# Routed mixture: seven sequences chosen and placed ahead of the tiles, and 85 tiles in one stream

## The chip, the cores and the metric

The kernel is one program on one core of a Trainium2 chip. The metric is device time in microseconds (us) of one launch. One execution was also taken by the hardware profiler; its trace is what the views below are read from.

## The reference, cut to what matters

The model carries eight sequences of 512 tokens by 128 features through ten layers: rwkv, attention, mixture, alibi, attention, mixture, lightning attention, **routed mixture**, differential attention, **routed mixture**. Only the routed mixture (layers 8 and 10, both with the same weights) is changed. It computes, in the reference's terms (tokens x after a layer norm):

```
logits = norm(x) @ w_gate                       # 8 experts
two largest logits -> softmax of the two        # TOP_K = 2
x += sum over the two chosen experts e of
     weight * ((silu(z @ w1[e]) * (z @ w3[e])) @ w2[e])
```

with w1, w3 of 128 by 256 and w2 of 256 by 128 for each of the eight experts. 4096 tokens, two experts each, make 8192 rows of expert work.

## The kernel before, in words

**Sorting instead of masking.** `routed_block` writes each token's normalized row twice into a DRAM buffer, sorted by expert, reads it back in tiles of 128 rows that all belong to one expert, runs the expert on the tile, writes the results, gathers each token's two result rows, and adds them with their weights. The eight sequences are cut into three chunks of 3, 3 and 2 sequences (`Routed.SEQS`); each chunk has its own sorted buffer, results buffer and table, and 31, 31 and 23 tiles (`Routed.TILES`: two rows per token, and seven tiles more for experts that fill no whole tile), 85 in all.

**What is done to a sequence j.** VectorE: `statistics` (mean and variance), `shifted`; GpSimd: `token_scales`, a power for a group of sequences (`Routed.SCALED`: 1; 2; 3 and 4; 5 to 7); ScalarE: `tokens`, the normalized rows; TensorE: `head_turned`, four transposes; ScalarE `head_hi` and VectorE `head_lo` split them in a high and a low half; TensorE `gate`, eight small products; VectorE `chosen`: the two largest logits of each token, their index and one-hot rows, and `both`, the sum of the one-hots; TensorE `ranks`: how many rows of each expert come before a token, by products of `both` with a triangle and with ones; VectorE `placed`: the row in the sorted buffer (`row_idx`), and the running fill `run`; GpSimd `sort`: eight indirect DMAs that write the rows. After the last sequence of a chunk, VectorE `tabled` makes from the fill the table of tiles (which expert, which row), and `way_back` the indices of the gathers.

**What is done to a tile n.** SyncE `tile` loads it (ten slots, `SLOTS`); TensorE turns it (L4727); ScalarE copies it (L4822); TensorE `up` (L4735, w1 and w3 at once); ScalarE silu (L4828); VectorE `product_g` (L4997); TensorE turns g (L4743); ScalarE copies (L4834); TensorE `down` (L4751, two products); VectorE `result` (L5004) copies it into one of four slots for pairs of tiles; SyncE `pair` (L4648) stores pairs.

**Order.** Each engine runs its list strictly in the order written, and waits on semaphores. TensorE's list per tile is up(n), down(n-2), turn of tile n+2, turn of g(n-1); VectorE's is result(n-2), product_g(n). Ahead of tile 0 stand the gates, ranks and choices of sequences 0 to 4 (`AHEAD` = 5). Sequences 5, 6 and 7 are fitted in among the tiles of chunk 0 from tiles 1, 8 and 15 on (`WITHIN`, `due`): gate and next turn, choice, low half, ranks, placing, and the table, in six consecutive turns. Each chunk's loop has two more turns than tiles (`turns`), in which its last tiles drain; the next chunk begins with its table's expert and two turned tiles:

```
wait(t, vec_table, c, "row")
at_w = {0: expert_of(0)}
tile_turned(n0)
tile_turned(n0 + 1)
for i in turns(c):
```

SyncE, per chunk: `pads` (eight stores that blank the row after each expert's fill), the pairs up to eight tiles before the chunk's first, a wait for the sort, then per tile the load and the pairs up to twelve tiles back. GpSimd: scales 0 and 1, sort 0, sort 1, scales 2, sort 2, scales 3, sorts 3 to 7, one power for all weights (`seconds`), and then 64 gathers (`gathered`, L5119), those of a chunk behind its last stored pairs. VectorE adds the sequences back (`added`, L5011 and L5015) at tiles 45, 52, 59, 76 and 83, and the last three behind the stream. In the first of the two layers, `opening` prepares the next layer; in the last one, SyncE stores the finished sequences (`tokens_out`).

Of the kernel before, what the change touches and what calls it, by code (L numbers as in the profile page):

```python
# [18 lines left out]
F32 = mybir.dt.float32  # L19
# [8 lines left out]
P = 128  # L28
# [4477 lines left out]
class Routed:  # L4506
# [13 lines left out]
    ADDED = {(1, 14): 0, (1, 21): 1, (1, 28): 2, (2, 14): 3, (2, 21): 4}  # L4520
    WITHIN = {5: (0, 1), 6: (0, 8), 7: (0, 15)}
    OPENED = 2
    AHEAD = 5
# [8 lines left out]
def routed_block(core, name, store):  # L4532
# [7 lines left out]
    PARTS = 6  # L4540
    WAY_BACK = 4
    chunk_of = lambda j: max(c for c in range(R.CHUNKS) if R.FIRST[c] <= j)
    last_of = lambda c: R.FIRST[c] + R.SEQS[c] - 1
    with ExitStack() as ctx:
# [5 lines left out]
        pe_rank, vec_shift, vec_table = steps("_ranks_tensor"), steps("_shift_vector"), steps("_table_vector")  # L4550
# [18 lines left out]
        both, place, picked = sb("both", [P, NQ * 8], F32R), sb("place", [P, NQ, 8]), sb("picked", [P, 2 * NQ, 8])  # L4569
        row_at, row_idx, run = sb("row_at", [P, NSEQ, 2 * NQ]), sb("row_idx", [P, NSEQ, 2 * NQ], U32), sb("run", [P, 8])  # L4570
# [23 lines left out]

        def due(c, i):

            for j, (of, first) in R.WITHIN.items():
                if of == c and first <= i < first + PARTS:
                    return j, i - first
            return None, None  # L4600

        turns = lambda c: range(R.TILES[c] + 2)
# [16 lines left out]
        def _(sp):  # L4619
# [47 lines left out]
            for c in range(R.CHUNKS):  # L4667
# [7 lines left out]
                for t in range(R.TILES[c]):  # L4675
                    tile(c, t)
                    if n0 + t >= 12:
                        m = pairs_to(m, n0 + t - 12)
                    if store and (c, t - SLOTS - 1) in R.ADDED:
                        tokens_out(R.ADDED[c, t - SLOTS - 1])  # L4680
                        shown.append(R.ADDED[c, t - SLOTS - 1])
# [8 lines left out]
        def _(t):  # L4690
# [17 lines left out]
            def ranks(j):  # L4708
                pe_rank.start()
                if j == 0:  # L4710
                    t.wait_ge(fixed, 5)
# [548 lines left out]
```

## Time and profile before

| | |
|---|---|
| runs timed | 3: 2580.46, 2586.67, 2590.57 us; median 2586.67 |
| profiled execution, own time | 2577.03 us |
| its span, first to last instruction | 2574.9 us |
| TensorE busy | 2186.4 us (85%) |
| VectorE busy | 1669.4 us (65%) |
| ScalarE busy | 1275.9 us (50%) |
| GpSimd busy | 1389.3 us (54%) |
| mean granted TensorE clock | 0.908 |
| first routed mixture | from about 1543 to 1804 us of the span |
| second routed mixture | from about 2317 us to the end |

Times in rows are us from the span's start. PE is TensorE, DVE VectorE, ACT ScalarE, POOL GpSimd, SPq SyncE's queue; PEclk is the granted clock as a share of full speed. Busy shares are means over ten unlike layers; the change is inside two of them.

### The profile page before, as it was taken

Reading aid. Unit: us, or ns where it says so; the run is one execution under the profiler, and the core shown is the slowest. Engines: PE = TensorE matmul, PEld = TensorE weight load, DVE = VectorE, ACT = ScalarE, POOL = GpSimd, SP = SyncE. Lnnn points to the kernel's source line nnn. Section 1 sums busy time; section 2 is a strip of 40 time slices with the busy share of each in tenths; the row PEclk is TensorE's granted clock in tenths of the full one; section 3 lists DMA queues with packets and bytes.
Section 4 is the critical chain, followed back from the end, with each engine's and each line's share of the span. In section 5 each row is a group of like instructions: output and inputs, shape, how many; then the busy total and the mean of one; then the engine's idle time right before and its main releaser. Section 6 shows DMA issues by size and latency. Waiting matters only on the chain. (4 is left out here: it accounts for less than half of the span.)

```text
span 2574.9 us, 41201 instructions
## 1 busy us (share of the span) xinstructions
PE 2186.4 (85%) x11902; PEld 1314.4 (51%) x11902; DVE 1669.4 (65%) x4560; ACT 1275.9 (50%) x2246; POOL 1389.3 (54%) x1353
## 2 busy tenths in 40 slices
PE   4567998999779979998999995984899999985894
PEld 3344565666665646664444444653444444434663
DVE  6865775677557747766666655543687877755543
ACT  4543454333344543335766643453477767763452
POOL 5933754343336544426666656445666766627435
PEclk8788798899788999999999995997899999995997
DMA  1000110322011111221000003332000000003333
GB/s 50 0 3 16 46 44 3 124 86 80 20 30 39 38 52 75 99 81 42 1 1 1 1 2 117 90 105 75 13 1 1 1 1 0 1 1 114 92 108 104
DMA packets 113863, 113.22 MB, mean 44 GB/s; under 512 B 22776, under 2 KB 93560, under 8 KB 113400
## 3 DMA queue, kind: packets, MB, share of 16 engines
q1 hardware_dynamic: 105464, 93.92, 12.1%
q0 software_dynamic: 8192, 16.79, 2.3%
q8 instruction: 99, 1.62, 0.3%
q14 instruction: 108, 0.88, 0.1%
HBM read 72.50 MB, written 25.43 MB: 38 GB/s over the span
## 5 line engine op out<-in xcount | busy, mean ns | idle before, releaser
L2332 DVE TENSOR_REDUCE l_diffneg_max<-psum 128x1 fp32r<-128x512 f32 x512 | 335.5, 685 | 89.6 <-PE psum L2070 86.0
L2247 ACT ACTIVATE l_diffweights<-psum 128x1024 f32<-128x1024 f32 x256 | 261.8, 1025 | 127.5 <-PE psum L2099 126.4
L2070 PE MATMUL psum<-l_diffkz,l_diffQ 128*128 128x512 f32 (+1 forms) x512 | 234.4, 476 | 3.2 <-DVE l_diffneg_max L2332 2.1
L2871 ACT ACTIVATE l_lightswapped<-psum 32x512 f32<-32x512 f32 x304 | 178.7, 588 | 101.1 <-DVE l_lightturned L2963 97.7
L1597 DVE TENSOR_REDUCE l_attn0neg_max<-psum 128x1 fp32r<-128x512 f32 x256 | 167.4, 683 | 51.5 <-PE psum L1328 48.8
L5119 POOL DMA_INDIRECT l_moe1yb<-results,l_moe1back_idx x128 | 122.7, 958 | 134.1 <-DVE l_moe1back_idx L4991 57.7
L1503 ACT ACTIVATE l_attn0weights<-psum 128x1024 f32<-128x1024 f32 x128 | 130.2, 1022 | 116.1 <-PE psum L1350 116.0
L4296 ACT ACTIVATE l_moe0s<-psum 128x512 f32<-128x512 f32 x144 | 85.8, 596 | 200.0 <-PE psum L855 183.0
L1724 POOL TENSOR_TENSOR l_attn0half_sums<-l_attn0weights 128x2048 f32<-128x2048 f32 x30 | 137.2, 4574 | 86.9 <-ACT l_attn0weights L1503 86.9
L4735 PE MATMUL psum<-l_moe1w,l_moe1zt 128*128 x340 | 183.8, 624 | 0.0
L5107 POOL DMA_INDIRECT sorted<-l_moe1rows,l_moe1row_idx x128 | 124.0, 969 | 79.9 <-DVE l_moe1run L4939 44.1
L175 POOL TENSOR_TENSOR settled<-powers 128x1 f32<-128x1 f32 x97 | 24.2, 250 | 257.9 <-DVE l_alibimv L702 70.7
L223 POOL TENSOR_TENSOR l_moe0ex<-powers,l_moe0hot 128x32 f32<-128x32 f32 x14 | 76.1, 5439 | 156.6 <-DVE l_moe0hot L274 156.6
L4751 PEld LDWEIGHTS psum<-l_moe1w,l_moe1gt 128*128 128x128 f32 x680 | 95.7, 193 | 121.0 <-issue 121.0
L4217 PE MATMUL psum<-l_moe0g,l_moe0w_raw 128*128 128x512 f32 x288 | 148.9, 602 | 7.5 <-ACT l_moe0out_sb L4271 7.5
L2070 PEld LDWEIGHTS psum<-l_diffkz,l_diffQ 128*128 128x128 f32 (+1 forms) x512 | 95.1, 186 | 111.5 <-issue 64.2
L5004 DVE COPY l_moe1y<-psum 128x128 f32<-128x128 f32 x170 | 49.4, 291 | 149.1 <-PE psum L4751 143.5
L2485 POOL TENSOR_TENSOR l_difflow_rows<-l_diffwhole,l_diffmarks 128x512 fp32r<-128x512 f32 x63 | 65.5, 1040 | 139.1 <-ACT l_diffwhole L2231 136.5
L2113 PE MATMUL psum<-l_diffweights,x 128*32 128x512 f32 x1024 | 137.0, 608 | 0.0
L4751 PE MATMUL psum<-l_moe1w,l_moe1gt 128*128 x680 | 108.5, 283 | 27.5 <-DVE l_moe1y L5004 22.4
L4371 DVE TENSOR_TENSOR l_moe0sc<-l_moe0s,l_moe0bcs 128x512 f32<-128x512 f32 x128 | 93.6, 731 | 58.5 <-ACT l_moe0s L4296 48.2
L2099 PE MATMUL psum<-l_diffQ,l_diffkz 32*128 32x512 f32 (+1 forms) x512 | 129.5, 494 | 1.5 <-DVE l_diffneg_max L2332 0.9
(602 smaller groups left out, 6055.7 us busy)
## 6 DMA issues: line engine op xcount, KB each, us to landing
l_moe0bcs<-gate_rows SPq DMA_DIRECT2D x64, 512.0 KB
l_moe1xt<-sorted SPq DMA_DIRECT2D x170, 64.0 KB, 1.8
results<-l_moe1y SPq DMA_DIRECT2D x82, 128.0 KB, 2.0
l_attn0Q<-l_attn0q_hi SPq DMA_DIRECT2D x128, 64.0 KB, 2.0
l_moe1w<-in_moe_w SPq DMA_DIRECT2D x6, 1024.0 KB, 8.8
l_attn0Q<-l_attn0q_lo SPq DMA_DIRECT2D x64, 64.0 KB, 2.0
sorted<-l_moe1spare SPq DMA_DIRECT2D x54, 64.0 KB, 1.6
l_moe0w_raw<-in_moe_w SPq DMA_DIRECT2D x20, 128.0 KB, 4.7
```

The lines of the kernel that those rows point to most:

```text
L1503: nc.scalar.activation(weights[:, tt, 2 * pair:2 * pair + 2, :], ps[:, S[m % 2]:S[m % 2] + 2, :], ACT.Exp, scale=SCALE).then_inc(act_exp.s ...
L1597: nc.vector.tensor_reduce(neg_max[:, n % 2, st, hh:hh + 1], ps[:, bank_of(("max", n, b)), :], AXX, ALU.max, negate=True).then_inc(vec_max. ...
L1724: nc.gpsimd.tensor_tensor(halves[:, a, :, :], weights[:, 2 * a, :, :], weights[:, 2 * a + 1, :, :], ALU.add).then_inc(pool_sum.sem, pool_s ...
L2070: nc.tensor.matmul(ps[:, bank, :], Q[rows, n % 4, st * P:(st + 1) * P], kz[rows, n % 4, hh, :], start=True, stop=True).then_inc(pe_max.sem ...
L2099: ins = nc.tensor.matmul(ps[:, S[m % 2] + h, :], kz[rows, n % 4, hh, tt * P:(tt + 1) * P], Q[rows, n % 4, :], start=True, stop=True)
L2113: ins = nc.tensor.matmul(ps[strip(hh), O, :], V[:, j % 2, tt, g * PER_GROUP + hh, :], weights[:, tt, hh, :], start=(tt == 0), stop=(tt == ...
L2247: nc.scalar.activation(weights[:, tt, 2 * pair:2 * pair + 2, :], ps[:, S[m % 2]:S[m % 2] + 2, :], ACT.Exp, scale=SCALE).then_inc(act_exp.s ...
L2332: nc.vector.tensor_reduce(neg_max[:, n % 2, st, row:row + 1], ps[:, bank_of(("max", n, b)), :], AXX, ALU.max, negate=True).then_inc(vec_ma ...
L2871: copy = lambda to, frm: nc.scalar.activation(to, frm, ACT.Copy)
L4217: ins = nc.tensor.matmul(ps[:, OUT, :], weights_in.raw[:, c:c + P], g[:, n % G_RING, h, :], **ends)
L4735: nc.tensor.matmul(ps[:, H[n % 2], :], zt[:, n % 2, :], w[:, bass.ds(w_at, 4 * P)], start=True, stop=True).then_inc(pe_up.sem, pe_up.step( ...
L4751: ins = nc.tensor.matmul(ps[:, Y, 0:P], gt[:, n % 2, h * P:(h + 1) * P], w[:, bass.ds(w_at + (4 + h) * P, P)], start=h == 0, stop=h == 1)
```

## The change

- `chosen`, `ranks` and `placed` of sequences 0 to 6 stand ahead of tile 0, and so do the gate and turn of sequence 7. Among the tiles remain the choice of sequence 7 (tile 1), its ranks (tile 3) and placing (tile 4), the tables of chunks 1 and 2 (tiles 6 and 10) and the ways back (tiles 2, 13, 16). `WITHIN`, `due` and `turns` go.
- `placed` gets a semaphore of its own (`vec_place`) and a fill per chunk (`run[:, c, :]`); the next choice waits for the ranks to have read `both`, and no longer for the placing. The copy of `base` into `run` goes.
- The tiles are one loop of 85 on TensorE, ScalarE and VectorE; only two drain turns at the end remain. The wait for a chunk's table stands where its first expert is read.
- `ranks` takes five products in place of eight: `both` has eight zero columns behind it, and the totals come out of the same products.
- GpSimd: scales 2 between sort 0 and sort 1, scales 3 between sort 1 and sort 2. VectorE: the statistics come earlier in the list, table 0 stands behind the choice of sequence 3, and the shifts of 5 to 7 behind table 0.
- SyncE: pairs are stored ahead of the load in a tile's turn, not behind it; finished sequences are stored eleven tiles after their adding back across chunks, so that in the last layer three, not one, are stored among the tiles.

```diff
+    ALL = sum(TILES)
+    CHOSEN, RANKED, PLACED = 1, 3, 4
+    TABLED = {6: 1, 10: 2}
+    WAYS_BACK = {2: 0, 13: 1, 16: 2}
+    ADDED = {45: 0, 52: 1, 59: 2, 76: 3, 83: 4}
...
                 for t in range(R.TILES[c]):
-                    tile(c, t)
                     if n0 + t >= 12:
                         m = pairs_to(m, n0 + t - 12)
+                    tile(c, t)
...
-                wait(t, chooser.vec_gate, j - 1, "comb")
+                wait(t, vec_place, j - 1, "comb")
                 wait(t, chooser.vec_gate, j, "both")
-                nc.tensor.matmul(ps[:, RANKS, 0:32], less[:, :], both[:, :], start=True, stop=False, skip_group_check=True)
-                for q in range(1, NQ):
-                    nc.tensor.matmul(ps[:, RANKS, 8 * q:32], ones[:, :], both[:, 0:32 - 8 * q], start=False, stop=q == NQ - 1,
-                                     skip_group_check=True)
-                for q in range(NQ):
-                    ins = nc.tensor.matmul(ps[:, RANKS, 32:40], ones[:, :], both[:, 8 * q:8 * q + 8], start=q == 0, stop=q == NQ - 1,
+                nc.tensor.matmul(ps[:, RANKS, 0:40], less[:, :], both[:, :], start=True, stop=False, skip_group_check=True)
+                for q in range(1, NQ + 1):
+                    ins = nc.tensor.matmul(ps[:, RANKS, 8 * q:40], ones[:, :], both[:, 0:40 - 8 * q], start=False, stop=q == NQ,
                                            skip_group_check=True)
...
             head_turned(3)
             gate(3)
+            ranks(2)
             head_turned(4)
-            ranks(3)
             gate(4)
-            ranks(4)
             head_turned(5)
...
+            for j in (4, 5, 6):
+                ranks(j - 1)
+                gate(j + 1)
+                if j + 2 < NSEQ:
+                    head_turned(j + 2)
+            ranks(6)
+            at_w = {}
+            for n in range(R.ALL):
...
+                up(n, at_w[n])
...
+                if n >= 2:
+                    down(n - 2, at_w.pop(n - 2))
+                if n + 2 < R.ALL:
+                    tile_turned(n + 2)
+                if n >= 1:
+                    g_turned(n - 1)
+                if n == R.RANKED:
+                    ranks(NSEQ - 1)
...
             placed(0)
+            statistics(3)
             head_lo(1)
             shifted(2)
-            statistics(3)
             statistics(4)
             chosen(1)
             head_lo(2)
+            statistics(5)
             placed(1)
+            shifted(3)
+            shifted(4)
+            statistics(6)
+            statistics(7)
+            head_lo(3)
             chosen(2)
             placed(2)
+            head_lo(4)
+            chosen(3)
             tabled(0)
...
             for j in range(5, NSEQ):
                 shifted(j)
...
+            for j in (4, 5, 6):
+                head_lo(j + 1)
+                chosen(j)
+                placed(j - 1)
+            placed(6)
+            for n in range(R.ALL):
+                if n >= 2:
+                    result(n - 2)
+                product_g(n)
+                if n == R.CHOSEN:
+                    chosen(NSEQ - 1)
+                if n == R.PLACED:
+                    placed(NSEQ - 1)
+                if n in R.TABLED:
+                    tabled(R.TABLED[n])
+                if n in R.WAYS_BACK:
+                    way_back(R.WAYS_BACK[n])
...
             sort(0)
+            token_scales(2)
             sort(1)
-            token_scales(2)
-            sort(2)
             token_scales(3)
-            for j in range(3, NSEQ):
+            for j in range(2, NSEQ):
                 sort(j)
```

## Rows read from the trace of the kernel before

**Rows 1.** Time line, VectorE, first mixture: products of tiles 0, 30, 32, 44, 61, 63. Columns: start, duration, engine, line, operation, tiles, count, [idle before, releaser].

```profile
1600.96 0.42 DVE L4997 TENSOR_TENSOR l_moe1g<-l_moe1s,psum 128x256 f32<-128x256 f32 x1 [3.86 <-ACT l_moe1s L4828]
...
1665.41 0.41 DVE L4997 TENSOR_TENSOR l_moe1g<-l_moe1s,psum 128x256 f32<-128x256 f32 x1
...
1671.89 0.42 DVE L4997 TENSOR_TENSOR l_moe1g<-l_moe1s,psum 128x256 f32<-128x256 f32 x1 [0.58 <-PE psum L4743]
...
1691.46 0.41 DVE L4997 TENSOR_TENSOR l_moe1g<-l_moe1s,psum 128x256 f32<-128x256 f32 x1
...
1726.75 0.41 DVE L4997 TENSOR_TENSOR l_moe1g<-l_moe1s,psum 128x256 f32<-128x256 f32 x1
...
1733.25 0.42 DVE L4997 TENSOR_TENSOR l_moe1g<-l_moe1s,psum 128x256 f32<-128x256 f32 x1 [0.58 <-PE psum L4743]
```

**Rows 2.** Time line, VectorE, second mixture: products of tiles 20, 30 and 31.

```profile
2420.43 0.41 DVE L4997 TENSOR_TENSOR l_moe1g<-l_moe1s,psum 128x256 f32<-128x256 f32 x1
...
2438.61 0.41 DVE L4997 TENSOR_TENSOR l_moe1g<-l_moe1s,psum 128x256 f32<-128x256 f32 x1
...
2445.04 0.42 DVE L4997 TENSOR_TENSOR l_moe1g<-l_moe1s,psum 128x256 f32<-128x256 f32 x1 [3.37 <-ACT l_moe1s L4828]
```

**Rows 3.** Windows: the head of the first mixture; clock behind POOL's busy time.

```profile
1543.00:1598.00 55.00, 23.58 (x101) 21.23 (x101) 32.56 (x253) 14.37 (x34) 38.38 (x44) 0.51 0.40 123
```

**Rows 4.** Time line, GpSimd, first mixture: first sort, second scale, last gathers.

```profile
1552.77 1.24 POOL L5107 DMA_INDIRECT sorted<-l_moe1rows,l_moe1row_idx  x1 [1.46 <-DVE l_moe1run L4939]
...
1572.97 1.70 POOL L5093 TENSOR_TENSOR l_moe1scale<-l_moe1var,powers 128x8 f32<-128x8 f32 x1
...
1774.99 0.94 POOL L5119 DMA_INDIRECT l_moe1yb<-results,l_moe1back_idx  x1 [5.18 <-DMA results<-l_moe1y]
```

**Rows 5.** Time line, VectorE, head of the first mixture: table 0 to sequence 3.

```profile
1571.11 0.17 DVE L4946 CAST l_moe1table<-l_moe1run 128x8 int32<-128x8 f32 x1
...
1574.77 0.28 DVE L4891 SCALAR_TENSOR_TENSOR l_moe1shift<-l_moe1mv,l_moe1scale 128x4 f32<-128x4 f32 x2
...
1578.51 0.69 DVE L4897 TENSOR_TENSOR l_moe1h_lo<-psum,l_moe1h_hi 128x512 fp32r<-128x512 f32 x1 [3.46 <-ACT l_moe1h_hi L4816]
...
1581.17 0.19 DVE L262 COPY l_moe1ex<-psum 128x32 f32<-128x32 f32 x1 [1.97 <-PE psum L216]
...
1583.32 0.19 DVE L4906 TENSOR_TENSOR l_moe1both<-l_moe1hots 128x32 fp32r<-128x32 f32 x1
...
1585.61 0.19 DVE L4931 TENSOR_TENSOR l_moe1place<-psum,l_moe1run 128x32 f32<-128x32 f32 x1 [1.41 <-PE psum L4719]
...
1586.49 0.16 DVE L4939 TENSOR_TENSOR l_moe1run<-l_moe1run,psum 128x8 f32<-128x8 f32 x1
```

**Rows 6.** Time line, TensorE: ranks' last products; turn of tile 31, second mixture.

```profile
1584.51 0.99 PE L4719 MATMUL psum<-l_moe1both,l_moe1ones 128*128 128x8 f32 x4
...
2441.53 0.30 PE L4727 MATMUL psum<-ident,l_moe1xt 128*128 128x128 f32 x1 [0.20 <-issue]
```

**Rows 7.** Time line, VectorE, first mixture: products of tiles 2, 3, 6, 7, 9.

```profile
1605.69 0.41 DVE L4997 TENSOR_TENSOR l_moe1g<-l_moe1s,psum 128x256 f32<-128x256 f32 x1
...
1608.47 0.41 DVE L4997 TENSOR_TENSOR l_moe1g<-l_moe1s,psum 128x256 f32<-128x256 f32 x1
...
1613.91 0.41 DVE L4997 TENSOR_TENSOR l_moe1g<-l_moe1s,psum 128x256 f32<-128x256 f32 x1
...
1618.13 0.41 DVE L4997 TENSOR_TENSOR l_moe1g<-l_moe1s,psum 128x256 f32<-128x256 f32 x1
...
1624.64 0.41 DVE L4997 TENSOR_TENSOR l_moe1g<-l_moe1s,psum 128x256 f32<-128x256 f32 x1
```

**Rows 8.** Time line, SyncE, second mixture: pads of chunk 1, loads from tile 31 on.

```profile
2422.69 8.15 SPq L4634 DMA_DIRECT2D sorted<-l_moe1spare  x8
...
2433.30 7.71 SPq L4640 DMA_DIRECT2D l_moe1xt<-sorted  x7
```

**Rows 9.** Page, DMA issues: tile loads, KB each, us to landing.

```profile
l_moe1xt<-sorted SPq DMA_DIRECT2D x170, 64.0 KB, 1.8
```

More of the change, by code:

```diff
@@ L4919, in placed @@
             def placed(j):
-                inc, wait_for = chooser.steps(d, j)
-                wait_for("both")
-                if j in R.FIRST:
-                    if j:
-                        wait(d, vec_table, chunk_of(j) - 1, "pads")
-                    v.tensor_copy(run[:, :], base[:, :]).then_inc(chooser.vec_gate.sem, chooser.vec_gate.step("begin"))
-                else:
-                    d.sem_inc(chooser.vec_gate.sem, chooser.vec_gate.step("begin"))
-                wait_for("begin")
+                vec_place.start()
+                inc = lambda ins, *key: ins.then_inc(vec_place.sem, vec_place.step(*key))
+                wait_for = lambda *key: wait(d, vec_place, j, *key)
+                c = chunk_of(j)
+                ahead = base[:, :] if j in R.FIRST else run[:, c, :]
                 wait(d, pe_rank, j, "rank")
+                wait(d, vec_place, j - 1, "comb")
                 found = ps[:, RANKS, 0:32].rearrange("p (q e) -> p q e", e=8)
-                inc(v.tensor_tensor(place[:, :, :], found, run[:, :].unsqueeze(1).to_broadcast([P, NQ, 8]), ALU.add), "place")
+                inc(v.tensor_tensor(place[:, :, :], found, ahead.unsqueeze(1).to_broadcast([P, NQ, 8]), ALU.add), "place")
                 wait_for("place")
@@ L4938, in placed @@
                 inc(v.tensor_copy(row_idx[:, j, :], row_at[:, j, :]), "row_idx")
-                inc(v.tensor_tensor(run[:, :], run[:, :], ps[:, RANKS, 32:40], ALU.add), "comb")
+                inc(v.tensor_tensor(run[:, c, :], ahead, ps[:, RANKS, 32:40], ALU.add), "comb")
             def tabled(c):
@@ L4944, in tabled @@
                 wait_for = lambda key: d.wait_ge(vec_table.sem, vec_table.done(c, key))
-                wait(d, chooser.vec_gate, last_of(c), "comb")
-                inc(v.tensor_copy(table[:, c, PAD_AT:PAD_AT + 8], run[:, :]), "pads")
-                inc(v.tensor_tensor(count[:, :], run[:, :], base[:, :], ALU.subtract), "count")
+                wait(d, vec_place, last_of(c), "comb")
+                inc(v.tensor_copy(table[:, c, PAD_AT:PAD_AT + 8], run[:, c, :]), "pads")
+                inc(v.tensor_tensor(count[:, :], run[:, c, :], base[:, :], ALU.subtract), "count")
                 wait_for("count")
@@ new lines, in _ @@
+            for j in (4, 5, 6):
[3 more added lines that the diff above has]
+            placed(6)
+            for n in range(R.ALL):
+                if n >= 2:
[9 more added lines that the diff above has]
+                    way_back(R.WAYS_BACK[n])
+                if n in R.ADDED:
+                    if R.ADDED[n] == 0:
+                        weighed()
+                    added(R.ADDED[n])
+                    if opening and R.ADDED[n] == 0:
+                        wait(d, vec_add, 0, "second")
+                        opening.statistics(d)
+                if opening and n == R.ALL - 1:
+                    opening.low(d, TOK)
+                    opening.weights_low(d)
```

158 lines of the change are left out of this document (48 added, 110 removed).

## The prediction

> **What bounds the kernel now.** The change touches only the routed mixture, which runs twice among the ten layers. I read the time line of each engine inside these two stretches; over the whole span the mixture is hidden behind averages. Call g(n) the start of tile n's gated product on VectorE: it is the beat of the tile stream.
>
> [rows 1] give the first mixture. Between g(32) and g(44) a tile costs (1691.46 - 1671.89)/12 = 1.63 us; 85 tiles at that beat would be 139 us. The real stream is slower in two places. Tiles 0 to 30 take 1665.41 - 1600.96 = 64.45 us where 30 beats are 48.9: 15.5 us lost. And at each seam between chunks two beats take 6.48 and 6.50 us in place of 3.26. [rows 2] show the same in the second mixture, where the first seam is 6.43 us for one beat. So the bound is the stream on TensorE, plus what VectorE puts between tiles, plus the drain and refill at the seams. Ahead of it lies the head, up to g(0), in which TensorE is granted 0.51 of its clock, the 1.2 GHz level for nearly all of it, and waits for short steps [rows 3]. Behind it lies the tail: GpSimd gathers, 16 pieces that wait for the last result [rows 4].
>
> **The change part by part.**
>
> *The head.* Seven sequences instead of five are chosen, ranked and placed before tile 0, and the gate's products of the eighth are made there. Steps from [rows 5], all at the head's slow clock: from shift to the low half 1578.51 - 1574.77 = 3.74; the low half 0.69; choosing, 1583.32 + 0.19 - 1581.17 = 2.34; from there to placing 2.10; placing, 1586.49 + 0.16 - 1585.61 = 1.04; a table, 1574.77 - 1571.11 = 3.66. The ranks' last four products take 0.99 [rows 6], 0.25 each; three fewer make the 2.10 into 1.35. On GpSimd a sort piece costs (1572.97 - 1552.77)/16 = 1.26 and the second scale 1.70 [rows 4].
>
> In the new order the second scale stands behind sort 0 alone: 1552.8 + 8 x 1.26 + 1.70 = 1564.6. VectorE waits for it with shift 3. From there: 3.74 to the low half of 3 (1568.3), 0.69 + 2.34 choosing 2 (1571.4), 1.35 + 1.04 placing it (1573.8), about 0.8 for the next turn (my estimate, part of the 3.74), 0.69 + 2.34 choosing 3 (1577.6), 3.66 for table 0 (1581.3). Only now does shift 5 stand in VectorE's order, though its scale was ready about 1577 (eight pieces and a scale after 1564.6); this is the new wait, and tokens, turn, high and low half of 5 follow it: 3.74, 1585.0. Then three rounds of low half, choice and placing, each 0.69 + 2.34 + 1.04 and 0.3 of waits = 4.4: 1598.1. Ranks 6, 1.35: 1599.5. TensorE turns tile 0 behind it, and from turn to product at the slow clock takes 2445.04 - 2441.53 = 3.51 [rows 2, 6]: g(0) at 1603.0 against 1600.96. **The head costs 2.0 us more in each mixture.** Bounds: 2 less (no waits inside the rounds, the first 0.8 hidden), 6 more (0.3 of waits becomes 1.5). The sort of chunk 0 is not the limit: 24 pieces and both scales end near 1587, and the tile lands well before 1599.
>
> *Tiles 0 to 30.* Before, three sequences' gate, turn, choice, ranks and placing and two tables fell among them. Now: one choice, one set of ranks, one placing, two tables and all ways back. [rows 7] price them: a choice stretches its beat to 2.78, so +1.15; placing with a table makes 4.22, so +2.6; the second, shorter table I put at +2.3. The way back right behind the choice gets 0.5 (between 0 and its length, about 1.15); the other two lie alone and fit the gap that VectorE has in a beat. Ranks with five products at the full clock 0.7, placing 0.3, the first tiles at the slow clock 0.3. Sum 7.85. Chunk 0 then takes 48.9 + 7.85 = 56.8: **7.7 us less per mixture.** Bounds of the insertions: 4 (what is only VectorE's is caught up again) and 12.
>
> *The seams.* The turns of tiles 31, 32 and 62, 63 no longer wait for the drain. But the queue of SyncE is in order: pads of the next chunk, 8.15 us, and pairs stand ahead of load 31, which goes out 2433.30 - 2420.43 = 12.9 after g(20) [rows 2, 8]; 1.8 to landing [rows 9] makes 14.7. The turn is wanted 3.5 before g(31), which is g(20) + 11 x 1.63 = 17.9, so at 14.4. I take a bubble of 0.6 (0 to 2). First seam: 6.48 becomes 3.86, 2.6 gained; in the second mixture 6.43 becomes 2.2, 4.2 gained. Second seam: adding back two sequences lies between g(51) and g(62) and gives SyncE time, no bubble: 3.2 in each.
>
> *The rest.* Pairs ahead of loads, not behind: loads run ten tiles ahead, nothing. The placing step's own semaphore and the copy of the base that goes: some 0.2 per placing, in VectorE's slack or in the 0.3 above. In the last layer two more stores of tokens leave in mid-stream; that puts two issues of about 1 us (the pads' 8.15/8) on SyncE ahead of loads that have slack. The tail moves with the last result as long as the gathers of chunk 1 are done: they had 5.18 us to spare [rows 4], and the pair of tile 61 comes up to 3 us later against the stream, so 2 stay. The first adding back may wait for its gather: 0.3 in each mixture. The tail itself is unchanged.
>
> Sum: first mixture -2.0 + 7.7 + 2.6 + 3.2 = 11.5, second -2.0 + 7.7 + 4.2 + 3.2 = 13.1, less 0.6: **24 us**. Against the profiled execution's own 2577.0 (span 2574.9 and 2.1 around it) that is 2553. The median of the runs shown, 2586.7, lies 9.6 above it, as does most of their spread (2580.5 to 2590.6); I forecast in the median's terms: 2586.7 - 24 = **2563**.
>
> On the clock: the rows say that the head runs at 1.2 GHz [rows 3], and that two beats behind the first table took 1624.64 - 1618.13 = 6.51 instead of 3.26 [rows 7], in which a gate and a turn (about 1.5 at the full clock) leave 1.7 unexplained but by a fallen clock. The Trainium skill (TensorE: Matmul & The Clock Gate, "Part 1: The HAM clock gate") has the throttled state as the default, which activity releases; by that rule every table in the stream, whose stall empties TensorE, could cost such a fall, and the sum would be the 2570 of the first rival below. By the rows alone it is one fall for two tables, for I see none behind the second. In my sum the fall is left out against the shortened beats after a stall, which I left out too.
>
> **Rivals.**
> *The clock falls behind both tables.* 1.7 x 4 = 6.8 lost: 2570. For it the 6.51 above; against it that no gate and turn of small products now follows the stall.
> *SyncE holds the first seam open.* Pairs 18 to 23 wait behind the pads, and results 26 on wait for their slots; without the long beat that the table behind tile 20 gave, SyncE is late by up to 3 more in each mixture, and the adding back waits too: 8 lost, 2571. For it: 14.7 against 14.4 is no margin, and a shorter g(20) to g(31) makes it worse.
> *A shorter head.* Choosing ahead packs as the bounds allow and the insertions cost 5: 2586.7 - 24 - 8 - 4 = 2551.
> *The insertions cost as before.* Choice, way back, placing and table follow each other within ten tiles, and VectorE never recovers: chunk 0 keeps its 64.45. 15.4 lost: 2578.
> *The other side: a serial head.* In [rows 5] one sequence from low half to placed takes 1586.65 - 1578.51 = 8.1 us, and with its turn some 10. If the rounds of sequences 3 to 6 run one behind the other (the single buffer of ranks, the logits' bank), four rounds of 10 instead of 4.4 add 22 in a mixture that gains 12: 10 slower each, 2607. It decides from 7.4 us a round on. Against it: the choice no longer waits for the placing before it.
> *It does nothing measurable,* with some wait unseen at both ends: 2586.
>
> **How the numbers follow.** Chances: forecast 0.43 (its own range 2557 to 2568), clock 0.13, SyncE 0.11, shorter head 0.11, insertions 0.13, nothing 0.03, serial 0.06. A measurement of this kernel tells some 0.5%, 13 us, from no change. Faster by that: the first four, 0.78. Within it: 0.16. Slower: 0.06. The unknown costs span 10 to 33 us of gain, 2554 to 2577, and the runs' own spread adds 4 to 5 below: 2549 to 2577.
>
> **What would show it.** g(0) 2 us later after the layer's start; tiles 0 to 30 in about 57 us with two long beats, at tiles 6 and 10; two beats of 1.6 to 2.3 at tile 31 and none at 62; the last gathers starting about 12 us earlier in each mixture. A round in the head above 7 us, a long beat at each table followed by beats of 3 us, or 64 us for tiles 0 to 30 would make it wrong.

## The result, and the profile after

| | before | after |
|---|---|---|
| median, same chip | 2588.6 us (4 runs, 2580.5 to 2592.2) | 2553.9 us (4 runs, 2549.0 to 2558.9) |
| ratio, 95% interval | | 0.9879 (0.9844 to 0.9913) |
| the same again, another chip | 2582.1 us (17 runs) | 2553.5 us (4 runs), ratio 0.9904 (0.9871 to 0.9937) |
| profiled execution, its span | 2574.9 us | 2557.1 us |

The change makes the kernel 25 to 31 us faster by the two ratios; the forecast was 24 us of gain and a time of 2563, and the time came out 9 us lower. The repeat was expected at a ratio of 0.985 to 0.991 with mixtures 14 to 16 us shorter; they were 12.5 and 14.6 shorter.

The VectorE time line of the changed kernel, first mixture: products of tiles 0, 6, 7, 20, 29 to 32, 61, 63 and 84. These answer to [rows 1].

```profile
1596.99 0.42 DVE L4986 TENSOR_TENSOR l_moe1g<-l_moe1s,psum 128x256 f32<-128x256 f32 x1 [2.31 <-ACT l_moe1s L4824]
...
1608.45 0.41 DVE L4986 TENSOR_TENSOR l_moe1g<-l_moe1s,psum 128x256 f32<-128x256 f32 x1
1612.66 0.41 DVE L4986 TENSOR_TENSOR l_moe1g<-l_moe1s,psum 128x256 f32<-128x256 f32 x1
...
1635.52 0.41 DVE L4986 TENSOR_TENSOR l_moe1g<-l_moe1s,psum 128x256 f32<-128x256 f32 x1
...
1650.26 0.41 DVE L4986 TENSOR_TENSOR l_moe1g<-l_moe1s,psum 128x256 f32<-128x256 f32 x1
1653.11 0.41 DVE L4986 TENSOR_TENSOR l_moe1g<-l_moe1s,psum 128x256 f32<-128x256 f32 x1
1655.09 0.41 DVE L4986 TENSOR_TENSOR l_moe1g<-l_moe1s,psum 128x256 f32<-128x256 f32 x1
1656.73 0.41 DVE L4986 TENSOR_TENSOR l_moe1g<-l_moe1s,psum 128x256 f32<-128x256 f32 x1
...
1710.28 0.41 DVE L4986 TENSOR_TENSOR l_moe1g<-l_moe1s,psum 128x256 f32<-128x256 f32 x1
...
1713.55 0.41 DVE L4986 TENSOR_TENSOR l_moe1g<-l_moe1s,psum 128x256 f32<-128x256 f32 x1
...
1749.89 0.41 DVE L4986 TENSOR_TENSOR l_moe1g<-l_moe1s,psum 128x256 f32<-128x256 f32 x1
```

I cut each mixture at such rows, and count from its first own instruction on VectorE (1539.46 here, 1544.53 in the profile of before), since the whole mixture started 5 us earlier here. So the head is 1596.99 - 1539.46 = 57.53, tiles 0 to 30 take 1653.11 - 1596.99 = 56.12, and so on. A beat is the time from one tile's product to the next. Later in the text "the second profile of after" is that of the repeat. All in us:

| | before, 1st and 2nd mixture | after | after, second profile |
|---|---|---|---|
| head, to g(0) | 56.43, 56.38 | 57.53, 57.51 | 57.52, 57.50 |
| g(0) to g(30) | 64.45, 64.09 | 56.12, 55.07 | 58.98, 55.91 |
| first seam, g(30) to g(32) | 6.48, 7.94 | 3.62, 3.27 | 3.29, 3.27 |
| g(32) to g(61) | 54.86, 50.61 | 53.55, 51.59 | 53.35, 51.14 |
| second seam, g(61) to g(63) | 6.50, 6.52 | 3.27, 3.26 | 3.26, 3.27 |
| g(63) to g(84) | 36.33, 36.53 | 36.34, 36.23 | 36.20, 36.38 |
| whole | 225.05, 222.07 | 210.43, 206.93 | 212.60, 207.47 |

The two mixtures together are 29.8 us shorter, 27.1 in the second profile. The spans differ by 17.8 only: between the mixtures the first profile of after is 16 us longer than before. That stretch holds no line of the change. What is longer in it shows in windows of ten us of the changed kernel, near the end of the differential layer:

```profile
2251.00:2261.00 10.00, 9.10 (x39) 4.79 (x36) 5.75 (x10) 4.16 (x5) 0.00 (x0) 0.62 0.00 0
2261.00:2271.00 10.00, 9.39 (x44) 3.66 (x41) 4.59 (x9) 4.25 (x5) 0.00 (x0) 0.67 0.01 2
2271.00:2281.00 10.00, 9.94 (x34) 3.20 (x33) 5.24 (x9) 3.85 (x5) 0.00 (x0) 0.50 0.00 0
2281.00:2291.00 10.00, 9.95 (x35) 3.64 (x35) 3.58 (x22) 4.98 (x7) 1.02 (x1) 0.50 0.00 0
```

Columns: window, length, busy time (and count) of TensorE, its weight loads, VectorE, ScalarE and GpSimd, then granted clock, DMA share, GB/s. The clock is 0.50 to 0.67 for 40 us, at or near the 1.2 GHz level. In the second profile of after the same work had 1.00:

```profile
2251.00:2261.00 10.00, 9.15 (x60) 4.42 (x61) 8.51 (x16) 6.56 (x9) 6.67 (x8) 1.00 0.01 2
2261.00:2271.00 10.00, 9.39 (x65) 4.94 (x64) 7.04 (x11) 5.72 (x8) 0.00 (x0) 1.00 0.01 2
```

So the same kernel does both. In ten profiles on ordinary chips the stretch from the last product of the first mixture to the second mixture is 548.6 to 550.7 us in eight, and 564.9 and 565.2 in two. On the slower chip of the next section it is 548.7 and 551.5 in two profiles, and 560.5 and 561.3 with the same fallen clock in two. All four long ones are of the changed kernel or one made from it (four of eleven), none of the three with the order of before; that is too few to say whether the change makes it more likely. From here on kernels are compared mixture by mixture.

### The profile page after: what moved, and what is told of

It is laid out like the page before. It is cut to its first block and busy times, and to the rows that moved or that the text cites. A ratio compares the mean times of both kernels' runs of the same rounds, so it can differ in the third digit from the quotient of the medians.

```text
span 2557.1 us, 41101 instructions
## 1 busy us (share of the span) xinstructions
PE 2191.2 (86%) x11854; PEld 1309.7 (51%) x11854; DVE 1665.6 (65%) x4556; ACT 1277.3 (50%) x2246; POOL 1390.8 (54%) x1353
## 5 line engine op out<-in xcount | busy, mean ns | idle before, releaser
L2070 PE MATMUL psum<-l_diffkz,l_diffQ 128*128 128x512 f32 (+1 forms) x512 | 239.8, 487 | 2.1 <-DVE l_diffneg_max L2332 1.1
L2113 PE MATMUL psum<-l_diffweights,x 128*32 128x512 f32 x1024 | 143.8, 636 | 0.0
L1328 PE MATMUL psum<-l_attn0K,l_attn0Q 96*128 96x512 f32 x256 | 122.6, 517 | 7.2 <-DVE x L1619 1.7
```

Source lines behind the costliest of these rows:

```text
L2070: nc.tensor.matmul(ps[:, bank, :], Q[rows, n % 4, st * P:(st + 1) * P], kz[rows, n % 4, hh, :], start=True, stop=True).then_inc(pe_max.sem ...
L2113: ins = nc.tensor.matmul(ps[strip(hh), O, :], V[:, j % 2, tt, g * PER_GROUP + hh, :], weights[:, tt, hh, :], start=(tt == 0), stop=(tt == ...
```

## The experiments

Beside the first four (`b_stream`, `e_drain` and the first run each of placing first and of the old scale order), the kernel before ran at 2759.5 us: that chip was slower, and nearly all of it in the mixtures (299 to 319 us each in these four kernels). The last section says what was seen of it. Three of the four were run again on ordinary chips, and stand beside their first run.

**One stream alone, put into the kernel before.** Cut to the loop's form on TensorE; ScalarE and VectorE likewise, with the insertions where they were:

```diff
-            for c in range(R.CHUNKS):
...
-                wait(t, vec_table, c, "row")
...
-                tile_turned(n0)
-                tile_turned(n0 + 1)
-                for i in turns(c):
...
+            for n in range(ALL + 2):
...
+                    if n + 1 in R.FIRST_TILE:
+                        wait(t, vec_table, R.FIRST_TILE.index(n + 1), "row")
```

> The kernel before, with its 85 tiles as one stream and nothing else of the change (sequences 5 to 7 still chosen among the tiles, placing as before, eight products). Theory (drain and refill are what a seam costs): from the layer's start to the product of tile 0 stays 56.4 us; tiles 0 to 30 stay at 64 us; from the product of tile 30 to that of 32 falls from 6.5 and 7.9 to 3.3 to 4.0, from 61 to 63 from 6.5 to 3.3; about 6 us less in the first mixture, 8 in the second. Rival (SyncE's queue with eight pads ahead of the next load sets the seam): the first seam stays above 5.4 us, and the two mixtures together gain less than 7 us.

Slower chip: ratio 0.9958 (0.9932 to 0.9983), all four seams 3.27. Again, on an ordinary chip:

> The kernel before with one part alone: all 85 tiles as one stream, nothing else changed. Theory: both seams of each mixture shrink from 6.5 to 7.9 us to two beats, 3.3 us, so 3.2 + 3.2 in the first mixture and 4.7 + 3.2 in the second, 14 us in all: ratio 0.9945 (0.993 to 0.9965), 2574 us where before takes 2588; head and tiles 0 to 30 stay at 56.4 and 64.4. Rival (SyncE holds the seam, as its loads stand behind eight pads): the first seam stays above 5 us and only the second shrinks, 7 us in all, ratio 0.9973.

Ratio 0.9955 (0.9930 to 0.9979). VectorE, tiles 30, 31, 32 of the first mixture:

```profile
1672.55 0.41 DVE L5001 TENSOR_TENSOR l_moe1g<-l_moe1s,psum 128x256 f32<-128x256 f32 x1
1674.22 0.41 DVE L5001 TENSOR_TENSOR l_moe1g<-l_moe1s,psum 128x256 f32<-128x256 f32 x1
1675.86 0.41 DVE L5001 TENSOR_TENSOR l_moe1g<-l_moe1s,psum 128x256 f32<-128x256 f32 x1
```

The seam is two ordinary beats. The seams were 3.31, 3.27, 3.27, 3.27; head (56.45, 56.38) and tiles 0 to 30 (64.46, 64.47) stayed. The mixtures are 216.57 and 215.40: 15.2 us of the change's 27 to 30. SyncE did not hold the seam here; I take it that the table, which in this kernel stands behind tile 20 (a beat of 3.91), gave it the time.

**The reverse: the changed kernel with the drain and refill at each seam.** The three loops of 85 tiles become three chunks again, on all three engines; nothing else is changed.

> The kernel after, with the chunks' drains and refills put back on TensorE, ScalarE and VectorE, all else as after. Theory: tile 0 at 57.5 us and tiles 0 to 30 in 55 to 56 us stay, both seams go back to 6.5 (up to 8 in the second mixture); 6 to 8 us more per mixture than after, so that choosing ahead alone is worth 7 to 8 us per mixture against before. Rival (the gain of tiles 0 to 30 comes with the loop's form): tiles 0 to 30 go back above 60 us.

Slower chip: ratio 0.9984 (0.9965 to 1.0004), against 0.9958 for the stream alone. Seams 8.05, 7.86, 6.64, 7.89 in place of 3.3; g(31) waits with VectorE idle for 3.00 us. The seams follow the drain in both directions. The rest of this expectation was missed on that chip: tile 0 stood at 74.2 and 73.7, tiles 0 to 30 took 74.7 each, and against the kernel before choosing ahead without the stream gained nothing that the times can tell, where 14 to 16 us had been expected. The drained kernel did not run on an ordinary chip, so what choosing ahead is worth alone rests on a difference, given in the next section.

**Placing ahead of choosing, in the last three rounds of the head.**

```diff
                 head_lo(j + 1)
-                chosen(j)
                 placed(j - 1)
+                chosen(j)
```

> The kernel after, with placing j-1 ahead of choice j in the three rounds of the head instead of behind it. Theory (a round of 4.63 us is a chain over TensorE: the gate's products wait for the logits to be read, then turn, high half, low half): the placing's 1.04 us now delays the logits, rounds become 5.7, tile 0 comes 3 us later, near 60.6 us. Rival (VectorE has idle time in each round and the placing fits into it): tile 0 at most 0.7 us later.

On the slower chip its single run took 2743.5 us, with g(0) at 81.4 and 74.9 us; heads of the changed kernel's form were stretched there in any case (74.2 and 73.7 in the drained one), so it decides nothing. Again:

> The changed kernel with the last three rounds of the head turned: placing j-1 stands ahead of choosing j, so the ranks' product and its wait come before the next choice. Theory (the new order gains by letting TensorE rank a sequence while VectorE chooses the next; without it choice, ranks and placing follow one another, 0.7 to 1.4 us of ranks in each of three rounds): g(0) comes 2 to 4 us after the changed kernel's 57.5, so 59.5 to 61.5, and each mixture is as much longer; ratio to the changed kernel 1.0015 to 1.003. Rival (the rounds are bound by TensorE's chain from gate to the next high half, in which VectorE waits anyway): g(0) within 0.7 of 57.5.

g(0) at 59.50 and 59.34, 2.0 and 1.8 later; mixtures 214.15 and 210.85; ratio to before 0.9916 (0.9896 to 0.9936). VectorE, low half of sequence 6 and what follows; first of this kernel, then of the changed one:

```profile
1591.58 0.69 DVE L4888 TENSOR_TENSOR l_moe1h_lo<-psum,l_moe1h_hi 128x512 fp32r<-128x512 f32 x1 [1.48 <-ACT l_moe1h_hi L4812]
1592.19 0.18 DVE L4920 TENSOR_TENSOR l_moe1place<-psum,l_moe1run 128x32 f32<-128x32 f32 x1
1595.35 0.19 DVE L4898 TENSOR_TENSOR l_moe1both<-l_moe1hots 128x32 fp32r<-128x32 f32 x1
1597.23 0.69 DVE L4888 TENSOR_TENSOR l_moe1h_lo<-psum,l_moe1h_hi 128x512 fp32r<-128x512 f32 x1 [1.70 <-ACT l_moe1h_hi L4812]
```

```profile
1583.58 0.69 DVE L4888 TENSOR_TENSOR l_moe1h_lo<-psum,l_moe1h_hi 128x512 fp32r<-128x512 f32 x1 [0.65 <-ACT l_moe1h_hi L4812]
1586.33 0.19 DVE L4898 TENSOR_TENSOR l_moe1both<-l_moe1hots 128x32 fp32r<-128x32 f32 x1
1586.44 0.18 DVE L4920 TENSOR_TENSOR l_moe1place<-psum,l_moe1run 128x32 f32<-128x32 f32 x1
1588.21 0.69 DVE L4888 TENSOR_TENSOR l_moe1h_lo<-psum,l_moe1h_hi 128x512 fp32r<-128x512 f32 x1 [0.74 <-ACT l_moe1h_hi L4812]
```

A round is 1597.23 - 1591.58 = 5.65 here against 1588.21 - 1583.58 = 4.63. Placing does not wait for the ranks; what waits is the next low half. In TensorE's list the next turn stands behind the gate, and the gate waits until the choice has read the logits before it (the TensorE rows of the ranking run below show that wait). With the 1.04 of placing ahead of the choice [rows 5] all that comes as much later: 5.65 - 4.63 = 1.02 a round, twice 2.0. So the first of the two expectations had the mechanism and the length of a round (5.7), and counted it three times where it shows twice. The second, that ranks would follow the choice in the open, was wrong in place; the size it gave was at its lower end.

**GpSimd's order of before, in the changed kernel.**

```diff
             sort(0)
-            token_scales(2)
             sort(1)
+            token_scales(2)
+            sort(2)
             token_scales(3)
-            for j in range(2, NSEQ):
+            for j in range(3, NSEQ):
```

> The kernel after, with GpSimd's scales in their old places (scales 2 behind sort 1, scales 3 behind sort 2). Theory (the head hangs on scale 2, for which VectorE waits with the shift of sequence 3): one sort of 8 pieces of 1.26 us more ahead of it, so the product of tile 0 comes 10 us later, at 67 to 68 us from the layer's start, in both mixtures; tiles 0 to 30 unchanged at 55 to 56. Rival (the head is bound by its rounds of choices behind table 0, and scale 2 has slack): tile 0 at most 3 us later, below 61.

Slower chip, a single run: 2770.8 us, the second mixture's g(0) at 87.2 where the drained kernel had 73.7. Again:

> The changed kernel with GpSimd in the order of before: sort 0, sort 1, scale 2, sort 2, scale 3. Theory (VectorE stands at shift 3 until scale 2 is there, and a sort of eight pieces is 8 x 1.26 = 10.1 us): scale 2 comes 10 us later, scale 3 as well, and g(0) comes at 66 to 70 in place of 57.5; each mixture 9 to 12 us longer, ratio to the changed kernel 1.007 to 1.0095. Rival (sequences 3 to 7 have slack behind the sort, which is then earlier by a scale): g(0) at 60 or less.

g(0) at 73.43 and 73.22; ratio to before 1.0019 (0.9999 to 1.0040). That is 15.9 and 15.7 us later, where theory and rival had 8.5 to 12.5 and 2.5 at most, and it eats the whole change. The waits of VectorE for a scale in the first head, of this kernel and then of the changed one (us in total, times, longest):

```profile
DVE l_moe1shift L4882 <- POOL l_moe1scale L5080: 19.2, 2, 13.4
```

```profile
DVE l_moe1shift L4882 <- POOL l_moe1scale L5080: 3.3, 1, 3.3
```

There are two waits where I had counted one. The time line of GpSimd in this kernel shows the second:

```profile
1573.02 1.69 POOL L5080 TENSOR_TENSOR l_moe1scale<-l_moe1var,powers 128x8 f32<-128x8 f32 x1
1584.57 1.04 POOL L5094 DMA_INDIRECT sorted<-l_moe1rows,l_moe1row_idx  x1 [9.86 <-DVE l_moe1run L4928]
...
1594.48 2.30 POOL L5080 TENSOR_TENSOR l_moe1scale<-l_moe1var,powers 128x12 f32<-128x12 f32 x1
```

Scale 2 comes behind sort 1, 10.1 later. Then sort 2 stands ahead of scale 3, and it waits 9.86 for sequence 2 to be placed, which itself hung on scale 2; scale 3 ends at 1596.8 and VectorE waits 5.8 more for it. 10.1 + 5.8 = 15.9.

**Eight products per ranking.** The first product again has 32 columns, three products of `ones` follow, and the totals get four of their own, as in the kernel before:

```diff
-                for q in range(1, NQ + 1):
-                    ins = nc.tensor.matmul(ps[:, RANKS, 8 * q:40], ones[:, :], both[:, 0:40 - 8 * q], start=False, stop=q == NQ,
...
+                for q in range(NQ):
+                    ins = nc.tensor.matmul(ps[:, RANKS, 32:40], ones[:, :], both[:, 8 * q:8 * q + 8], start=q == 0, stop=q == NQ - 1,
```

> The changed kernel with eight products per ranking instead of five. Theory: three more products of 0.25 us each at the head's low clock, on the path from choosing to placing only once behind the last choice (ranks 6) and hidden behind the next choice in the other rounds: g(0) 0.75 later (58.2), nothing among the tiles; 1.5 to 2 us in all, ratio 1.0006, not to be told from 1 by the times. Rival (TensorE carries the rounds): 0.75 in each of three rounds and behind them, g(0) at 60 to 60.5.

g(0) at 59.27 and 59.24, 1.74 later; ratio to before 0.9896 (0.9873 to 0.9919), so the time can't tell it from the changed kernel, the trace can. Mixtures 212.86 and 210.14. The 1.74 lies between what the two theories gave, but the rows decide for the first: the rounds did not grow. VectorE, low halves of sequences 5, 6 and 7 in this kernel:

```profile
1582.23 0.69 DVE L4891 TENSOR_TENSOR l_moe1h_lo<-psum,l_moe1h_hi 128x512 fp32r<-128x512 f32 x1 [3.44 <-ACT l_moe1h_hi L4815]
1586.87 0.69 DVE L4891 TENSOR_TENSOR l_moe1h_lo<-psum,l_moe1h_hi 128x512 fp32r<-128x512 f32 x1 [0.65 <-ACT l_moe1h_hi L4815]
1591.50 0.69 DVE L4891 TENSOR_TENSOR l_moe1h_lo<-psum,l_moe1h_hi 128x512 fp32r<-128x512 f32 x1 [0.74 <-ACT l_moe1h_hi L4815]
```

A round is 4.64 and 4.63 here, and 4.63 in the changed kernel. The three products show where the placing has to wait for the ranks: 0.64 at the first placing of the head, 0.6 between the low halves of sequences 3 and 4 (6.67 against 6.04), and 0.64 behind the last low half (9.42 against 8.78 to g(0)); 0.2 comes back around table 0. The theory had only the last of the three. TensorE's time line in the changed kernel, one round, from the turn to the end of the ranks and on to the next gate:

```profile
1581.80 1.11 PE L4690 MATMUL psum<-ident,l_moe1rows 128*128 128x128 f32 x4
1582.99 0.40 PE L4705 MATMUL psum<-l_moe1both,l_moe1less 128*128 128x40 f32 x1
1583.22 1.00 PE L4707 MATMUL psum<-l_moe1both,l_moe1ones 128*128 128x32 f32 x4
1584.74 0.35 PE L215 MATMUL psum<-open_gate,l_moe1h_hi 128*128 128x16 f32 x1 [0.52 <-DVE l_moe1logits L264]
```

The ranks stand ahead of the gate, and the gate ahead of the next turn. In the gap of 0.52 TensorE waits for VectorE to have read the logits, and what is added to the ranks goes into that gap. So a round is a chain over three engines: low half and logits on VectorE, gate and turn on TensorE, high half on ScalarE, then the next low half, for which VectorE is idle 0.65 to 0.74. The ranks are beside it.

**Shifts 5 to 7 ahead of table 0.** `tabled(0)` moves from ahead of the loop that shifts 5, 6, 7 to behind it.

> The changed kernel with shifts 5 to 7 ahead of table 0 on VectorE, nothing else. Theory (my own step: shift 5 behind table 0 is the new wait of the head; scale 3 is there at about 1571 and table 0 ends at 1575): g(0) comes 3 to 4 us earlier, at 53.5 to 54.5, as in the version with four alterations (53.3 and 53.1), and the rest of the mixture is unchanged; each mixture 3 to 4 us shorter, ratio to the changed kernel 0.997 to 0.9977. Rival (the gain there came from reading the logits earlier in the rounds): g(0) at 57.

g(0) at 54.00 and 53.84, 3.5 and 3.7 earlier; mixtures 206.29 and 203.77, 4.1 and 3.2 less than the first profile of after; ratio to before 0.9890 (0.9863 to 0.9917). That is 0.9986 of the changed kernel by the repeat, where 0.997 to 0.9977 was expected; the times can't tell the two apart, the trace can. VectorE, changed kernel and then this one (a table's last instruction, the shifts, the next low half; the shifts, the table's first instruction, the next low half):

```profile
1575.13 0.17 DVE L4964 SCALAR_TENSOR_TENSOR l_moe1offset<-l_moe1first_tile,l_moe1base 128x8 f32<-128x8 f32 x1
1575.21 0.31 DVE L4882 SCALAR_TENSOR_TENSOR l_moe1shift<-l_moe1mv,l_moe1scale 128x4 f32<-128x4 f32 x3
1578.95 0.69 DVE L4888 TENSOR_TENSOR l_moe1h_lo<-psum,l_moe1h_hi 128x512 fp32r<-128x512 f32 x1 [3.42 <-ACT l_moe1h_hi L4812]
```

```profile
1577.62 0.30 DVE L4882 SCALAR_TENSOR_TENSOR l_moe1shift<-l_moe1mv,l_moe1scale 128x4 f32<-128x4 f32 x3
1577.84 0.16 DVE L4935 CAST l_moe1table<-l_moe1run 128x8 int32<-128x8 f32 x1
...
1581.57 0.68 DVE L4888 TENSOR_TENSOR l_moe1h_lo<-psum,l_moe1h_hi 128x512 fp32r<-128x512 f32 x1
```

Behind the shift nothing but the chain to the next low half is left, 3.4 us of idle time; with the shifts ahead, the table fills it.

**Tables 1 and 2 in five parts.**

```diff
-    TABLED = {6: 1, 10: 2}
-    WAYS_BACK = {2: 0, 13: 1, 16: 2}
+    TABLED = {6: 1, 11: 2}
+    WAYS_BACK = {2: 0, 17: 1, 19: 2}
...
-                    tabled(R.TABLED[n])
+                    parts = table_parts(R.TABLED[n])
+                if min(R.TABLED) <= n < max(R.TABLED) + 5:
+                    next(parts)
```

> The changed kernel with the tables of chunks 1 and 2 cut into five parts each, one part behind each of tiles 6 to 10 and 11 to 15; the ways back of chunks 1 and 2 move behind tiles 17 and 19. Theory (a table is dear because its VectorE work of about 3.5 us stands in one piece, while each beat has some 0.7 us to spare): the beats of 4.2 at tile 7 and 3.8 at tile 11 fall to under 2.1 each, tiles 0 to 30 take 51 to 53 us in place of 56, each mixture 3 to 5 us less, ratio to the changed kernel 0.9965 to 0.998 (6 to 9 us). Rival (what VectorE gets in between delays the product g of each tile, since it runs in order): each of the ten beats grows by 0.4 or more, tiles 0 to 30 take 55 us or more, ratio 0.999 to 1.001.

Median 2543.5, ratio to before 0.9864 (0.9831 to 0.9897), to the changed kernel on the same chip 0.9864/0.9904 = 0.996. Tiles 0 to 30 take 52.67 and 51.61. Windows by beat, this kernel, from g(6) to g(8), with the columns of the windows above:

```profile
1614.63:1616.27 1.64, 1.64 (x11) 1.12 (x11) 1.12 (x8) 0.99 (x4) 1.11 (x2) 1.00 0.39 119
1616.27:1617.97 1.70, 1.70 (x11) 1.18 (x10) 1.29 (x7) 1.06 (x4) 1.31 (x2) 1.00 0.59 178
```

and of the second profile of after, from g(6) to g(9), first mixture:

```profile
1613.80:1618.03 4.23, 2.57 (x12) 1.22 (x10) 3.92 (x20) 1.87 (x6) 3.22 (x4) 1.00 0.29 90
1618.03:1619.30 1.27, 0.95 (x7) 0.95 (x8) 0.61 (x3) 0.10 (x1) 0.96 (x1) 0.91 0.37 115
1619.30:1622.37 3.07, 3.07 (x11) 2.04 (x10) 0.63 (x4) 0.95 (x3) 2.26 (x3) 0.50 0.37 114
```

With a part in it VectorE is busy for 1.1 to 1.3 us of a beat, and the beat stays at 1.64 and 1.70; in one piece it is 3.92 busy in a beat of 4.23, and TensorE runs dry. In that execution the clock then fell to 0.50 and a beat took 3.07.

**Four alterations together:** tables in parts, shifts ahead of table 0, the logits of a round read ahead of the next low half, and one pad of chunks 1 and 2 behind every second tile of the chunk before:

```diff
+                    first = 16 if c == 0 else 10
+                    if c + 1 < R.CHUNKS and t >= first and (t - first) % 2 == 0 and (t - first) // 2 < 8:
+                        pads(c + 1, (t - first) // 2)
```

> The changed kernel with four alterations: tables in five parts (as the run before), shifts 5 to 7 ahead of table 0 instead of behind it, the pads of chunks 1 and 2 issued one every second tile of the chunk before them, and in each of the last rounds the logits read ahead of the next low half. Theory: parts save 4 us a mixture; the shifts fill the 3.3 us in which VectorE waits for scale 2, which brings tile 0 2 to 3 us forward; the pads take the beats at tiles 28 to 31 from 2.9 to 1.7 us, 1 to 2; the rounds 0.5 each. Some 8 to 10 us a mixture, 16 to 20 in all: ratio to the changed kernel 0.992 to 0.994, to before 0.978 to 0.982. Rival (the last rounds are held by TensorE's chain of turn, high half and product, not by where VectorE's shifts stand): tile 0 comes at the same time, and 4 to 5 us a mixture are left, ratio to the changed kernel 0.996 to 0.997.

Median 2527.5 us (2520.9 to 2533.9, 6 runs), ratio to before 0.9797 (0.9770 to 0.9823), to the changed kernel 0.9797/0.9904 = 0.9892: by the medians 26 us below the changed kernel and 55 below the one before. The mixtures are 199.79 and 197.37. The head is 53.28 and 53.11: by the run with the shifts alone 3.6 comes from the shifts, and what is left, 0.7, I put to the logits, which were not moved alone. With them a round is 4.25 in place of 4.63. No beat from tile 18 to 33 is above 1.75 us. The gain over the changed kernel is more than the 0.992 to 0.994 that was expected. It is the fastest kernel of this study.

## Why the prediction was right, and where its terms were off

The gain was forecast well, the time less so: 2553.9 us lies inside the whole range (2549 to 2577), but below the forecast's own 2557 to 2568 and nearest to the rival of a shorter head at 2551, which did not happen: the head was longer, and chunk 0 took 7.2 and 6.2 us beyond plain beats (10.1 and 7.0 in the second profile), where that rival had 5.

**The head: +2.0 forecast, +1.1 measured in all four mixtures.** In the first profile's times, moved by the 5.1 that the layers ahead were shorter, shift 5 stood at 1580.3 (forecast 1581.3) right behind table 0, as the working had it. That is the 1 us, and 0.7 of it was there already at scale 2 (1563.9, forecast 1564.6). The rounds are 4.63, not 4.4 (+0.7 in three): the working added up VectorE's own steps and 0.3 of waits, where the rows show the chain over three engines described above. From the last low half to g(0) it took 0.7 less than the working had, which gives that back; the two errors cancelled by luck. That shift 5 behind the table is the new wait was the right step, and it is shown: 3.6 us, by the run that moved it. What the head hangs on above all is a step that the working passes in one line and never priced the other way round, scale 2 behind sort 0 alone: 15.9 us. The range "2 less, 6 more" holds the result.

**Tiles 0 to 30: -7.7 forecast; -8.3 and -9.0 measured, -5.5 and -8.2 in the second profile.** The first 31 took 56.1, forecast 56.8. The beats are those of the price list of [rows 7]: 4.21 at tile 7 (table 1, forecast +2.6, measured +2.6), 3.76 at tile 11 (table 2: forecast +2.3, measured +2.1), 2.90 at tile 2 (choice and way back: 1.65 forecast, 1.27 measured). So here the sum by beats worked. A beat of 1.28 to 1.29 behind each table (tiles 8 and 12) gives back 0.35, and the working had left that out on purpose, against the fall of the clock.

**The first seam: -2.6 and -4.2 forecast; the seam itself gave -2.9 and -4.7, and the bubble was there, but ahead of it.** Queue of SyncE and TensorE's turns, changed kernel:

```profile
1637.79 8.53 SPq L4625 DMA_DIRECT2D sorted<-l_moe1spare  x8
1646.65 1.43 SPq L4639 DMA_DIRECT2D results<-l_moe1y  x3
1649.05 6.78 SPq L4631 DMA_DIRECT2D l_moe1xt<-sorted  x6
```

```profile
1648.22 0.27 PE L4720 MATMUL psum<-ident,l_moe1xt 128*128 128x128 f32 x1
1650.92 0.33 PE L4720 MATMUL psum<-ident,l_moe1xt 128*128 128x128 f32 x1 [0.90 <-DMA l_moe1xt<-sorted]
```

Load 31 goes out 1649.05 - 1635.52 = 13.5 after g(20) (forecast 12.9, from [rows 8]) and is there 1.87 later (forecast 1.8). TensorE stands idle 0.90 for it ahead of its turn, and the beats of tiles 30 and 31 grow to 2.85 and 1.98, not those of 31 and 32. The beat of tile 28, 1.99, has another wait, of VectorE for a slot whose pair is not yet stored:

```profile
1648.77 0.29 DVE L4993 COPY l_moe1y<-psum 128x128 f32<-128x128 f32 x1 [1.37 <-DMA results<-l_moe1y]
```

The three beats are 1.9 above plain ones. In the second mixture it is 0.5 at tile 30 and 0.6 at 33, the latter again the wait for a stored pair (1.64 idle at 2432.64). Forecast: a bubble of 0.6, 0 to 2; the wait for the slot was in the rival's reasoning, not in the working's. In the run with four alterations both waits are gone, while the run with tables in parts alone keeps a beat of 3.45 at tile 30. So it is SyncE's queue at the chunk's start; but that run spreads the pads and also drops the three pair stores behind them, and it can't tell the 8.53 us of the one from the 1.43 of the other except by their size.

**The second seam: -3.2 forecast, -3.2 and -3.3 measured.** No bubble, as said.

**The rest.** Tiles 32 to 61 came out 1.3 shorter in the first mixture and 1.0 longer in the second; 0.3 longer each had been forecast. The last gathers wait 2.8 us for the last result (5.5 in the second profile), against 5.18 in [rows 4]; the forecast left them 2 to spare. They come 14.5 us earlier in the mixture, forecast 12.

**The sum.** 24 was forecast, the mixtures gave 29.8 and 27.1, and the ratios 31 and 25. Of the difference 1.8 is the head, and in the first profile 2.7 is tiles 0 to 30 and the first seam (in the second the fallen clock turned that into 0.6 the other way); the rest is inside what one execution differs from another.

**The rivals.** *Serial head:* even with placing put first, a round was 5.65, below the 7.4 from which it would have decided. *SyncE holds the first seam:* true by 1 to 2 us, with both of its waits, but not by 3 in each and without the adding back. *The clock falls behind both tables:* it happens, in some executions. In six profiles with both tables in one piece on ordinary chips (after twice, placing first, the old scale order, eight products, shifts ahead) 24 tables stood in the stream, and behind five of them a beat was 2.96 to 3.20 with the clock at 0.50 to 0.56; in the mixture where it fell behind both, it cost 58.98 - 56.12 = 2.9. The rival gave 1.7 for each table. The 1.7 that the prediction had read out of the kernel before was such a fall: the beat of 5.22 there (tile 9) has a clock of 0.51, the one of 4.61 in its second mixture 0.63. Part of what tiles 0 to 30 gained is that this fall mostly stays away. With tables in parts it did not happen in four mixtures. Of the rule weighed in the prediction (the Trainium skill, TensorE: Matmul & The Clock Gate, "Part 1: The HAM clock gate": activity releases the clock, throttled is the default), the rows of the mixtures show the fall only behind beats in which TensorE ran dry: behind five of the 24 tables, and in all six profiles behind the beat of 4.9 to 5.0 us at tile 46 in the first mixture (clock 0.50 to 0.66 at tile 47 or 48), but not behind the one of 3.6 to 3.8 in the second. The prediction's reading, a fall for some tables and not for all, holds. The 40 us at 0.50 to 0.67 in the differential layer do not fit so simply: TensorE was busy for 9.1 of 10 us or more in each window there, no less than with the clock at 1.00. *Insertions as before* and *nothing* did not come.

**How much each part is worth.** By mixture: the stream 15.2 for both together, by the kernel before with it alone. By difference, the other 12 to 15 are the insertions taken out of the stream, and with them the fall of the clock, less the longer head. The new order on GpSimd was not tried alone in the kernel before; the longer list ahead of tile 0 can only be had with it, for without it 31.6 us are lost. The five-product ranking is worth 3.5 us in the two heads (1.74 twice); over the whole mixtures the difference is 5.6 us against the first profile of after and 2.9 against the second.

## What to carry to other kernels

Where a list ahead of a stream grows, look for the engine that serves two of its steps in one order: a step of 1.7 us put behind eight issues of 1.26 us came 10 us later, and a second one behind a step that waited for the first cost 6 more. What is inserted into a stream that another engine bounds costs what it exceeds the gap by, so cut it into parts that fit (0.5 to 0.7 of 1.0 us free) rather than look for a better place; and spread the issues of a queue in the same way. A cost added to a step of a round is not paid where the round's chain passes it by: take two of the round's own rows before and after, rather than the sum at its end. Compare two profiles by stages that the change touches: their spans here differed by 16 us for a stretch that was the same code.

## What the runs showed of the chip that I had not expected

*The granted clock differs between executions of the same instructions.* A stretch of 40 us near the end of the differential layer ran at 1.00 in eight profiles and mostly at 0.50 to 0.67 in two, 15 to 16 us apart; nothing of the changed kernels is in that layer, and I can't say what decides it.

*One chip was slow in this layer alone.* The span up to the first mixture was as elsewhere (1543 us), but with the one stream in the kernel before a mixture took 306.5 and 302.3 us there, and 216.6 and 215.4 on an ordinary chip. What VectorE waited for there in that kernel, and the same wait of the kernel before on an ordinary chip (both from 1600 us to 1860; that kernel with the stream has the same, 71.8 in 66):

```profile
DVE l_moe1y L5008 <- remote: 75.9, 8, 19.0
DVE l_moe1y L5008 <- PE psum L4752: 64.1, 55, 2.6
```

```profile
DVE l_moe1y L5004 <- PE psum L4751: 72.6, 66, 4.6
```

The copy of a result out of PSUM waited eight times, 19 us at the longest, for something outside the engines' records. It is the instruction that needs a pair's slot to be stored; I take it for late stores, which the trace of that chip does not show landing. GpSimd's sort pieces were the same there (973 ns against 970 in the same stretch), so the issue on that engine was not slower. Why one chip does so stays open. There the seams closed as elsewhere, and the stream's ratio was the same, 0.9958 against 0.9955.
